# All five weight matrices over GpSimd's DMA queue with a cast on the way, and a list scheduler's latency of 380 in place of 450

## The reference

```python
x = x + attn(layernorm(x), Wq, Wk, Wv, Wo)     # x: [8, 4096, 1024] float32
x = x + einsum('bsi,oi->bso', layernorm(x), sign(Wf))

# attn: 16 heads of 64; q, k, v = x @ Wq.T, x @ Wk.T, x @ Wv.T
q, k = rope(q, k); q = elu(q) + 1; k = elu(k) + 1
# over time t, per head:
K_sum += k_t;  KV += k_t[:, None] * v_t[None, :]
y_t = (q_t @ KV) / max(q_t . K_sum, 1e-6)
# y @ Wo.T
```

## Time and profile before

| | |
|---|---|
| median of the timed runs | 1240.41 us |
| profiled execution, own time | 1252.24 us |
| its span (slowest core, core 4) | 1250.6 us |
| spans of cores 0 to 3 | 1232.5 to 1237.5 us, granted clock 0.891 to 0.896 |
| spans of cores 4 to 7 | 1245.8 to 1250.6 us, granted clock 0.834 to 0.843 |
| TensorE (PE) busy | 946.5 us, 76% |
| VectorE (DVE) busy | 700.6 us, 56% |
| ScalarE (ACT) busy | 508.6 us, 41% |
| GpSimd (POOL) busy | 158.2 us, 13% |
| DMA | 55.19 MB, of which the weights and tables 19.4 MB |

### The profile page before, as it was taken

How to read it: one execution, slowest core, us unless ns; L and a number is a source line. 1 busy time by engine, 2 the same in 40 slices (tenths; PEclk the granted TensorE clock), 3 DMA queues, 4 the chain that set the end, 5 groups by cost and what they waited for, 6 DMA issues and landing times.

```text
span 1250.6 us, 33867 instructions; the slowest of 8 cores (1232.5 to 1250.6 us)
## 1 busy us (share of the span) xinstructions
PE 946.5 (76%) x13571; PEld 868.2 (69%) x13571; DVE 700.6 (56%) x1530; ACT 508.6 (41%) x1007; POOL 158.2 (13%) x135
## 2 busy tenths in 40 slices
PE   0447777787777877878787778787888888888885
PEld 0336776677776766777676667776777887777885
DVE  4344556665555566655555666555556645456643
ACT  2237344444433444443434444434344343334341
POOL 0001011111110011111100111111001111001110
PEclk9857798998989898998989899898777777777775
DMA  9751000010000001101000010010001000101000
GB/s 227 227 186 53 35 19 36 36 35 19 35 36 35 19 36 35 36 19 35 36 35 19 35 36 35 19 36 35 21 33 36 36 18 35 35 19 36 19 6 31
DMA packets 15595, 55.19 MB, mean 44 GB/s; under 512 B 1872, under 2 KB 1872, under 8 KB 15440
## 3 DMA queue, kind: packets, MB, share of 16 engines
q1 hardware_dynamic: 11808, 42.01, 9.4%
q10 hardware_dynamic: 2304, 8.39, 2.0%
q0 software_dynamic: 1328, 2.62, 1.4%
HBM read 38.86 MB, written 16.78 MB: 44 GB/s over the span
## 4 chain that ended last, share of the span: by engine, by line
PE 29%; DVE 29%; issue 21%; ACT 12%; DMA 6%; DVEq 1%; POOL 1%; ACTq 0%; POOLq 0%; SPq 0%
PE pjA L515 6%; PE att L515 6%; PE pjB L515 6%; PE pjC L515 6%; DVE junkV L422 4%; DVE x L731 3%; DVE Asb L648 3%; DMA wq<-wqT 3%; DVE outb L747 3%; ACT qT L493 2%; ACT kev L529 2%; PE ptr L466 2%; DMA x<-wvT 2%; DVE ln L459 2%; ACT qT L496 1%
## 5 line engine op out<-in xcount | busy, mean ns | idle before, releaser
L545 POOL TENSOR_TENSOR rA<-qev,tabS_s 128x512 bf16<-128x512 bf16 x32 | 37.3, 1164 | 925.0 <-ACT qev L529 852.4
L515 PE MATMUL pjA<-wo,YT 128*128 128x128 bf16 x544 | 101.2, 262 | 6.6 <-ACT YT L719 6.6
L515 PE MATMUL att<-wo,YT 128*128 128x128 bf16 x544 | 100.3, 262 | 7.4 <-ACT YT L719 7.4
L515 PE MATMUL att<-wq,ln1T 128*128 128x128 bf16 x512 | 79.9, 237 | 23.5 <-DMA wq<-wqT 23.5
L515 PE MATMUL att<-wv,ln1T 128*128 128x128 bf16 x512 | 72.3, 230 | 30.5 <-DVE wv L361 16.3
L515 PE MATMUL pjC<-wo,YT 128*128 128x128 bf16 x480 | 89.1, 262 | 6.6 <-ACT YT L719 6.6
L515 PE MATMUL pjB<-wo,YT 128*128 128x128 bf16 x480 | 89.5, 261 | 5.8 <-ACT YT L719 5.8
L515 PE MATMUL pjB<-wf,ln2T 128*128 128x128 bf16 x512 | 80.7, 230 | 1.1 <-ACT ln2T L472 1.1
L515 PE MATMUL pjA<-wv,ln1T 128*128 128x128 bf16 x512 | 71.8, 229 | 12.4 <-ACT kev L529 12.4
L515 PE MATMUL pjA<-wf,ln2T 128*128 128x128 bf16 x512 | 80.2, 226 | 0.0
L515 PE MATMUL pjC<-wv,ln1T 128*128 128x128 bf16 x512 | 69.8, 225 | 13.2 <-ACT kev L529 13.2
(11 more groups left out here) (152 smaller groups left out, 3047.4 us busy)
## 6 DMA issues: line engine op xcount, KB each, us to landing
xs<-x SPq DMA_DIRECT2D x32, 512.0 KB, 3.7
out<-outb SPq DMA_DIRECT2D x32, 512.0 KB, 2.6
outb<-woT ACTq DMA_DIRECT2D x8, 512.0 KB, 10.2
x<-wkT SPq DMA_DIRECT2D x8, 512.0 KB, 11.1
x<-wvT SPq DMA_DIRECT2D x8, 512.0 KB, 5.7
outb<-wfT ACTq DMA_DIRECT2D x8, 512.0 KB, 4.7
wq<-wqT POOLq DMA_DIRECT2D x1, 2048.0 KB, 38.9
tabS_s<-tabS POOLq DMA_DIRECT2D x1, 256.0 KB, 42.8
```

The costliest lines, as they stand in the source:

```text
L515: s.add("tensor", lambda e, o=o, i=i, pj=pj, off=off, lsb=lsb, w_sb=w_sb: e.matmul(pj[:, off:off + 128], lsb[:, i * 128:(i + 1) * 128], w_ ...
L545: s.add("gpsimd", lambda e: e.tensor_tensor(out=rAv, in0=HI, in1=Sb, op=ALU.mult), reads=[src_res, "tabS"], writes=["rA"], tag=f"{tag}_rA")
```

## The change

The four groups of staged loads and casts go. Each weight is now loaded by one casting DMA from GpSimd, under one name per weight, and `sign_wf` waits for all of Wf. ScalarE issues no DMAs any more. `LAT` in the scheduler goes from 450 to 380, which changes the orders on all engines. The other lines take out environment knobs whose defaults were the values that now stand there (costs of 70 and 700, the mask and the division on VectorE); they change nothing by themselves.

```diff
-        LAT = float(os.environ.get("SIMLAT", 450.0))
+        LAT = float(os.environ.get("SIMLAT", 380.0))
...
-                 for e in ("sync", "gpsimd", "scalar") for j in range(3)}
+                 for e in ("sync", "gpsimd") for j in range(3)}
...
-        s.add("gpsimd",
-              lambda e: e.dma_start(
-                  out=wq[:].rearrange("p (a o) -> p a o", a=8),
-                  in_=wq_d.rearrange("(a p) o -> p a o", p=128)),
-              writes=[f"wqb{i}" for i in range(8)], dma=True,
-              tag="load_wq", cost=7000)
-        for wsb, wdram, name, qeng, ceng, stg in (
-                (wk, wk_d, "wk", "sync", "vector", x2),
-                (wv, wv_d, "wv", "sync", "vector", x2),
-                (wo, wo_d, "wo", "scalar", "scalar", outb),
-                (wf, wf_d, "wf", "scalar", "scalar", outb)):
-            for i in range(8):
-                sb = stg[i % 2]
-                sres = f"stg_{id(stg) % 97}_{i % 2}"
-                s.add(qeng,
-                      lambda e, sb=sb, b=wdram, i=i: e.dma_start(
-                          out=sb[:],
-                          in_=b.rearrange("(a p) o -> p a o", p=128)[:, i, :]),
...
-                s.add(ceng, fn, reads=[sres], writes=[f"{name}b{i}"],
-                      tag=f"cast_{name}p{i}", cost=800 if ceng == "vector" else 1400)
+        for wsb, wdram, name in ((wq, wq_d, "wq"), (wk, wk_d, "wk"),
+                                 (wv, wv_d, "wv"), (wo, wo_d, "wo"),
+                                 (wf, wf_d, "wf")):
+            s.add("gpsimd",
+                  lambda e, a=wsb, b=wdram: e.dma_start(
+                      out=a[:].rearrange("p (a o) -> p a o", a=8),
+                      in_=b.rearrange("(a p) o -> p a o", p=128)),
+                  writes=[name], dma=True, tag=f"load_{name}", cost=7000)
         s.add("scalar", lambda e: e.sign(wf[:], wf[:]),
-              reads=[f"wfb{i}" for i in range(8)],
-              writes=[f"wfb{i}" for i in range(8)], tag="sign_wf")
+              reads=["wf"], writes=["wf"], tag="sign_wf")
```

More of the change, by code:

```diff
@@ L163, in schedule @@
                 print(f"  {k:24s} n={v:5d}  t={hist_t[k]/1000:.1f}us")
[L164 to L171, removed]
         return order
@@ L324, in build_program @@
         bank_pool = [(att, "att"), (pjA, "pjA"), (pjB, "pjB"), (pjC, "pjC")]
-        for _f in range(int(os.environ.get("SIM_FAKEPOOL", 0))):
-            bank_pool.append((pjC, f"pjF{_f}"))
         bank_ctr = [0]
         def next_bank():
-            b = bank_pool[bank_ctr[0] % len(bank_pool)]
+            b = bank_pool[bank_ctr[0] % 4]
             bank_ctr[0] += 1
@@ L508, in emit_proj @@
             lresA, lresB = lres
-            wresi = [f"{wres}b{i}" for i in range(8)]
             banks = (next_bank(), next_bank())
@@ L519, in emit_proj @@
                         start=(i == 0), stop=(i == 7)),
-                        reads=[lresA if i < 4 else lresB, wresi[i]],
-                        writes=[pjres], tag=f"{tag}_o{o}i{i}", cost=MMC)
+                        reads=[lresA if i < 4 else lresB, wres],
+                        writes=[pjres], tag=f"{tag}_o{o}i{i}")
                 if o == 3:
@@ L645, in back_attn @@
                         start=True, stop=True, skip_group_check=True),
-                        reads=[qTh(h), kTh(h)], writes=[abres], tag=f"A{c}_h{h}",
-                        cost=MMC)
-                s.add(MASK_ENG, lambda e, g=g, ab=ab: e.tensor_tensor(
+                        reads=[qTh(h), kTh(h)], writes=[abres], tag=f"A{c}_h{h}")
+                s.add("vector", lambda e, g=g, ab=ab: e.tensor_tensor(
                     out=Asb[:, g * 512:(g + 1) * 512].rearrange("p (h t) -> p h t", t=128),
@@ L651, in back_attn @@
                     in1=mb, op=ALU.mult),
-                    reads=[abres, "mask"], writes=[f"A{g}"], tag=f"mask{c}_g{g}",
-                    cost=MASK_COST)
+                    reads=[abres, "mask"], writes=[f"A{g}"], tag=f"mask{c}_g{g}")
                 for hh in range(4):
@@ L702, in back_attn @@
                     reads=[f"r16a{p}"], writes=[f"r16b{p}"], cost=220)
-                s.add(YDIV_ENG, lambda e, nh=nh, h0=h0, pyv=pyv: e.tensor_tensor(
+                s.add("vector", lambda e, nh=nh, h0=h0, pyv=pyv: e.tensor_tensor(
                     out=Ysb[:, h0 * 64:(h0 + nh) * 64].rearrange("p (h e) -> p h e", e=64),
@@ L707, in back_attn @@
                     op=ALU.mult),
-                    reads=[ybres, f"r16b{p}"], writes=[f"Y{p}"], tag=f"ydiv{c}_p{p}",
-                    cost=YDIV_COST)
+                    reads=[ybres, f"r16b{p}"], writes=[f"Y{p}"], tag=f"ydiv{c}_p{p}")
                 for i in ytiles_after[p]:
```

29 lines of the change are left out of this document (4 added, 25 removed).

## The result

| | before | after |
|---|---|---|
| median | 1241.4 us (10 runs) | 1276.4 us (9 runs, 1272.5 to 1279.9) |
| ratio, 95% interval | | 1.0276 [1.0260, 1.0292] |
| profiled execution, own time | 1252.24 us | 1276.79 us |
| its span, slowest core | 1250.6 us, core 4 | 1274.9 us, core 2 |
| first store, mean of the 8 cores | 129.8 us | 119.6 us |

The kernel is 35 us slower; the forecast was 1241 us, with 1228 to 1257 as its range. The head won 10 us and the 31 chunks lost 45. Part 1 of the page hardly shows it: TensorE is busy 23 us longer than in the earlier trace rows, the other engines a little less.

The account below looks back on a forecast made before the run. No engine is full: the head waits for weights, then each chunk's path crosses all engines, with TensorE's clock part of the loop. Head -8.8 and chunks +9.6 give +0.8 on the median 1240.4: 1241 us, range 1228 to 1257.

Parts of the forecast that it names:

- The head: Stretch up to the first store, waiting for weights: first store at 124.0 instead of 132.76 us, 8.8 us gained.
- The gap ahead of Wo: In the head, Wo's load is issued late, behind `rA` and `rB`, which wait for `tabS`: 5.6 us.
- rival D: Weight queue slower than the mean: Wf lands at 103 to 109 us, head loses 6 to 12; chance 0.12.
- The path of a chunk: `kE` to first mask 1.05 us longer, 0.72 given back behind the masks: net +0.33 us a chunk.
- The split of the 1.05 us: Between `kE` and first mask: 0.2 us from the later `rstd`, the rest from the layer norm's application ahead of `kT`.
- The other moves: Earlier `ln2` application and transposes, `rD` of k ahead of `phi` of q: counted at nothing, 0.3 us either way.
- The clock: Whether TensorE's granted clock takes the 0.33 us a chunk or adds to it; three outcomes, +0 to +25 us.
- case A: The clock's pair pattern breaks at times; each chunk costs its own 0.33 us, 29 x 0.33 = +9.6 us; chance 0.38.
- the stretch at 0.50 ends at a fixed distance from its start: TensorE's slow clock: a chunk 1 us later spends 1 us less of Wo's products in it and gains 0.5 back.
- the long kind: Chunk with 10.24 us at clock 0.50 instead of 3.42; all chunks becoming so costs 0.55 us each.
- Case C: All chunks become of the long kind: +16 us, up to 25 with 0.33 on top, 1248 to 1257 us; chance 0.25.

Follow-up runs that it names:

- e1: Changed kernel's five casting loads with the scheduler's latency at the old 450, so chunks keep the old order: 1230.7 us, ratio 0.9911 to the kernel before.
- e3: Changed kernel plus 81 idle identity products a chunk where TensorE waits: 1181.7 us, ratio 0.9510 to the kernel before.
- e4: e1 plus the same 81 idle products a chunk in TensorE's waits as e3: 1178.9 us, ratio 0.9490 to the kernel before.
- e16: Changed kernel with only the layer norm's application put back behind the masks in chunks 2 to 28: 1244.1 us, ratio 1.0030 to the kernel before.
- e17: e16 with ScalarE's order of latency 450 as well: 1253.6 us, ratio 1.0078 to the kernel before.
- e11: Changed kernel plus 49 of e3's 81 products, ahead of v, around the transposes of `YT` and ahead of Wo: 1210.3 us, ratio 0.9753.
- e9: e1 plus four unused one-column VectorE operations ahead of the first copy of `kT`, chunks 3 to 29: 1240.1 us, ratio 0.9982 to the kernel before.
- e13: e1 plus two unused 128x1024 bfloat16 VectorE operations ahead of the first copy of `kT`, chunks 3 to 29: 1259.1 us, ratio 1.0151.
- e7: Changed kernel plus 32 of e3's 81 products, 16 ahead of the transposes of `kT` and 16 ahead of `A`: 1238.1 us, ratio 0.9972.

## Why the prediction was wrong, by its own steps

**The head: right.** Forecast -8.8 us; the cores' first stores come 10.2 us earlier on average (12.5 from the traced core of before to that of after) and e1 wins 9.7. Wf landed at 84.6 (88.1 forecast). A packet cost 0.798 x 16 x 90 / 5488 = 0.209 us (0.216 forecast). The gap ahead of Wo was there: 17.7 us from issue to landing, of which 1024 packets over 16 engines take 13.4. From the evacuation of `YT` behind the sign (91.57) to the store 28.7 us (28.9 forecast). The prediction's rival D, the slow queue, falls. The Trainium skill describes in "SBUF — State Buffer", section "SBUF: two separate sides", how a DMA of GpSimd starves while VectorE holds their common port. The prediction had priced such a stall at 5 us for each of Wk, Wv and Wf, from Wq's start; Wk and Wv landed 34.4 and 46.8 us behind their issues at 2.61 and 3.48, 13.3 us apart, which is the bare data. Wf landed 12.8 us behind Wo. No such stall shows in this trace.

**The path of a chunk: right in place and size.** 7.82 us from `kE` to the mask (7.81 forecast), no application behind the masks, no wait of the denominators at full clock. From `kE` to the denominators it takes 10.22 us instead of 9.88, 0.34 more (0.33 forecast); how little of it reaches the chunk at full clock, 0.09 us, e3 against e4 shows. The split of the 1.05 us to the mask was wrong: the prediction gave 0.2 to the later `rstd` and the rest to the application, but with the application back (e16) 0.44 of it is left, and with ScalarE's old order (e17) none of that comes back. The residual between the copies explains it by the rows.

**The other moves at nothing: open.** They weren't run alone. e16's rest of 13.4 us doesn't speak against them, since nearly all of it lies between `kE` and the mask.

**The clock: this step failed.** Asked whether the clock takes the 0.33 us or adds to it, the prediction let it add nothing in case A, 9.6 us in all; the 31 chunks lost 45, or 1.45 each. I took the fall of the clock as given and asked only where Wo starts behind it; I wrote that "the stretch at 0.50 ends at a fixed distance from its start", and took 10.24 us, "the long kind", as the worst a chunk can have. The move doesn't only make Wo later: it lengthens TensorE's wait ahead of `A` from 0.49 to 1.45 us, and the fall itself comes sooner, at the head of `A`, 8.3 us ahead of Wo. A fourth length appeared, 13.65 us, and the chunk settled on it. Case C was the right direction with the wrong size, 0.55 us a chunk and at most 0.88 with the chunk's own delay; between the stores 3 and 29 core 2 shows 37.56 - 35.83 = 1.73, core 0 36.81 - 35.83 = 0.98. I had the wait's price in the earlier trace rows (1.05 us more to the first mask) and never carried it over to TensorE, which waits for the same copies.

**What a stretch costs.** With 34.1 us a chunk at full clock, the 6.83 us of before cost 35.83 - 34.1 = 1.73, and core 2's 13.4 (mean between the stores 3 and 29) cost 37.56 - 34.1 = 3.46: 0.25 and 0.26 us for each us at 0.50. That isn't a constant: the same sum for core 0 gives 0.20 in e11, and 0.34 and 0.42 in e16 and e17, where the path is longer too. The Trainium skill, in "TensorE: Matmul & The Clock Gate", section "HAM oscillation — how this bites in real kernels", counts the loss at half of the slow time. Here it would be 6.7 us a chunk on core 2, twice what is measured: 7.5 of its 13.4 us lie ahead of the first product with Wo, mostly beside masks and divisions, and a mask takes 0.69 us at 0.50 as at 1.00. I also overlooked what this meant for before: 1.73 us in each of 31 chunks, 54 us, was there to be won (e4 against e1: 52), by far the largest item in its trace.

## What to carry to other kernels

When a trace shows TensorE's granted clock falling at the same place of every iteration, price each moved instruction also by what it does to TensorE's waits ahead of that place, even if the path gets the time back; 0.8 us moved cost 1.2 us a chunk here. Then try to close the waits: 81 idle products a chunk, placed in the waits, made this kernel 5.1% faster (e4, 1178.9 us, ratio 0.9490 [0.9459, 0.9521]), with what is said above on heads 14 and 15 still to be mended, while the same products in a dense place cost 65 us. Of the kernels without extra products e1 is the best, 0.9% under the one before. And measure a delay's dose in the wait that it is meant to lengthen before reading its price.

## What the runs showed of the hardware that was not expected

- The added one-column operations of VectorE take 0.14 us each in the trace, but four in a row delayed what follows by 0.24 us together, 0.06 each (e9); two of 128x1024 in bfloat16, 0.42 us each, delayed by 0.66 (e13). The 0.21 us that the doses were reckoned from is that of `st_nmr`.
- Chunk length and clock settle on each other: 37.5 us with 13.65 at 0.50, or 71.7 for two with 3.4 and 10.2. Cores with the same program hold different patterns in one execution (core 2: 324 us at 0.50 from 140 to 1090, core 0: 280), which makes a spread of 19 us between equal cores.
- The clock fell in a chunk with several short waits. The longest that TensorE has from 300 to 650 us in after is 1.9 us, by the view of waits (total, times, longest):

```profile
PE ptr L439 <- ACT qT L454: 14.1, 10, 1.4
PE ptr L662 <- DVE r16a L648: 5.7, 9, 0.8
PE pjC L472 <- ACT kev L486: 5.5, 3, 1.9
```

Closing either group of them (e7, e11) shortened the stretches.
